# Decoder kernel: four barrier-separated stages of a batch become one program, the output projection moves between two halves of the input projections

## The reference

```python
x = x + mamba(layernorm(x))                 # selective scan, 512 inner channels, 16 states
x = x + attention(layernorm(x), ctx)        # 16 heads: causal self plus cross, one projection Wp
x = x + ffn(layernorm(x))                   # abel = gelu(xn @ W); top-2 of 8 experts; rotation; gate
```

## Time and profile before

| what | us |
|---|---|
| median of 3 runs | 2071.34 (2068.38 to 2071.91) |
| the profiled execution's own time | 2069.24 |
| its span, first to last instruction | 2067.5 |
| PE busy in the span | 1588.2 (77%) |
| DVE busy | 1411.7 (68%) |
| ACT busy | 834.1 (40%) |
| POOL busy | 660.5 (32%) |
| mean granted clock of PE, share of full | 0.878 |

### The profile page before, as it was taken

One profiled execution on the slowest core, in us unless ns is written; L12 is line 12 of the kernel. 1 busy time (PEld: TensorE's weight loads), 2 busy tenths in 40 slices (PEclk: granted clock), 3 DMA queues, 4 the chain that ended last, 5 costly groups with the idle time before them and its releaser, 6 DMA issues. The chain is left out here.

```text
span 2067.5 us, 19892 instructions
## 1 busy us (share of the span) xinstructions
PE 1588.2 (77%) x6792; PEld 757.9 (37%) x6792; DVE 1411.7 (68%) x2092; ACT 834.1 (40%) x1570; POOL 660.5 (32%) x427
## 2 busy tenths in 40 slices
PE   4797699863987699773987799673567899759995
PEld 2454222231544222231544223231233232338884
DVE  5996878465996777276995877277987777234324
ACT  4542156624542166634442266452322466412221
POOL 2653401123663311114653311206654012122221
PEclk9899799985999699976998699886997799859998
DMA  5920721003002720012004520021006320116763
GB/s 170 295 84 13 178 41 20 2 0 129 0 1 66 146 40 1 1 44 86 1 0 115 98 39 2 1 82 42 0 0 144 48 39 2 63 64 220 254 198 124
DMA packets 121189, 147.46 MB, mean 71 GB/s; under 512 B 15429, under 2 KB 103886, under 8 KB 119040
## 3 DMA queue, kind: packets, MB, share of 16 engines
q1 hardware_dynamic: 117344, 137.53, 24.6%
q0 software_dynamic: 3744, 8.66, 1.2%
HBM read 96.79 MB, written 50.79 MB: 71 GB/s over the span
## 5 line engine op out<-in xcount | busy, mean ns | idle before, releaser
L168 PE MATMUL PS<-arena 128*32 128x512 f32 (+11 forms) x4150 | 884.6, 453 | 102.2 <-ACT arena L1698 23.4
L168 PEld LDWEIGHTS PS<-arena 128*32 128x32 f32 (+3 forms) x4150 | 368.5, 128 | 595.6 <-ACT arena L1698 276.0
L1698 ACT ACTIVATE arena<-PS 128x512 f32<-128x512 f32 (+3 forms) x768 | 375.4, 541 | 379.6 <-PE PS L168 378.4
L1328 POOL TENSOR_TENSOR arena<-arena 128x1024 f32<-128x1024 f32 x128 | 302.1, 2361 | 185.9 <-DVE arena L1352 147.1
L1718 DVE TENSOR_REDUCE maxs<-PS 128x1 f32<-128x1024 f32 x256 | 302.2, 1216 | 79.5 <-PE PS L168 79.4
L1352 DVE TENSOR_TENSOR_SCAN arena<-PS,arena 128x1024 f32<-128x1024 f32 x128 | 292.1, 2282 | 9.3 <-POOL arena L1328 9.3
L1308 ACT ACTIVATE PS<-arena,A_neg 128x511 f32<-128x511 f32 x256 | 166.0, 681 | 264.8 <-DVE arena L1352 194.4
L168 PE MATMUL PS<-arena,ident 128*128 128x512 f32 (+1 forms) x560 | 262.2, 595 | 5.4 <-DVE arena L1361 5.4
L1551 POOL TENSOR_TENSOR arena<-xn 128x512 f32<-128x512 f32 x16 | 20.3, 1266 | 586.4 <-ACT xn L1686 586.4
L168 PE MATMUL PS<-bc,bc_sel 96*128 96x512 bf16 x128 | 53.2, 416 | 153.5 <-DVE arena L1361 96.1
L1361 DVE TENSOR_TENSOR arena<-arena,PS 128x1024 f32<-128x1024 f32 x128 | 156.3, 1221 | 7.3 <-PE PS L168 3.2
(11 more groups left out here) (258 smaller groups left out, 1763.4 us busy)
## 6 DMA issues: line engine op xcount, KB each, us to landing
arena<-in_ew SPq DMA_DIRECT2D x46, 512.0 KB
arena<-stack_parts SPq DMA_DIRECT2D x288, 64.0 KB, 4.2
rows_in<-nil SPq DMA_DIRECT2D x16, 1088.0 KB, 12.0
arena<-b_rows SPq DMA_DIRECT2D x16, 1024.0 KB, 7.7
stack_parts<-arena SPq DMA_DIRECT2D x40, 384.0 KB, 3.1
arena<-stack_parts SPq DMA_DIRECT2D x96, 128.0 KB, 4.7
arena<-rows_in SPq DMA_DIRECT2D x23, 272.0 KB, 5.4
arena<-picked_rows SPq DMA_DIRECT2D x16, 256.0 KB, 3.2
```

The source lines that it names most:

```text
L168: return nc.tensor.matmul(o, l, r, start=start, stop=stop)
L1328: nc.gpsimd.tensor_tensor(b_sb[i % 2], u[:, 2 * kh:2 * kh + 2, :], Brow[:, n, :].unsqueeze(1).to_broadcast([P, 2, T]), ALU.mult).then_inc( ...
L1698: nc.scalar.activation(probs[(HG * s + h) % NPR][:, 0:N], bank(4 + n % 2)[:, 0:N], ACT.Exp, scale=HD ** -0.5).then_inc(S["ring_read"], 1)
```

## The change

There is one block a round, in which each engine runs its programs of the stages one after another: `[entry(0), scan(0)]` first, then `[queries(b), attention(b), entry(b + 1), scan(b + 1)]` for each b, the last without a scan. The barriers between queries, attention, entry and scan are gone; the one after the scan stays, and `reset()` stands there now. Where a barrier ordered something, a counter does: the rows in the diff with `wait_ge`. With it come:

- PE: the transposes of the new batch (from a new place, `xnE`) and the first four of the eight groups of input projections stand before `project`, the other four behind it.
- DVE: `normalise` of the new batch stands ahead of the last group's reciprocal, which moves from `attention` to `entry`; `conv(0)` and `conv(1)` stand before `residual`, `conv(2)` between `norm_first` and `norm_second`.
- `inputs` tells `u_ready` after each channel group, and POOL's products of the scan wait for two of them.
- POOL: the eight scatters of a batch stand one behind each of units 1 to 8 of the scan; only after batch 3 are they together. The add of the abel output (L821) is gone; in its place DVE adds it in the experts' phase, one add of 128x1024 a batch.
- Buffers are laid elsewhere (`xn2`, `dots`, the order of `GA2, GA3, GT, GA, GX`), the load of `GX` waits for `ab_mm`, and ACT for `res_added` and `kept` in units 1 and 5 of the scan.

```diff
-        for b in range(NB + 1):
+        def entry(b):
             begins, ends = b < NB, b >= 1
...
         def project():
+            pe.wait_ge(S["y_ready"], NG)
...
-                    if ends:
-                        project()
                     if begins:
-                        to_columns(pe, xn, 0, 0)
-                        pe.wait_ge(S["xT_ready"], 2)
+                    to_columns(pe, xnE, TT * ends, 0)
+                    pe.wait_ge(S["xT_ready"], 2 + 2 * ends)
+                    if ends:
+                        pe.wait_ge(S["ring_read"], ring_den(NG - 1, 1) + 1)
                         for m in range(2 * DT):
+                        if ends and m == DT:
+                            project()
...
-                            last = nc.vector.tensor_tensor(u[:, m, :], delta[:, m, :], xs[:, m, :], ALU.mult)
-                        link(last)
+                        nc.vector.tensor_tensor(u[:, m, :], delta[:, m, :], xs[:, m, :], ALU.mult)\
+                            .then_inc(S["u_ready"], 1)
...
-                        normalise(dve, link, x_sb, xn)
+                    normalise(dve, link, x_sb, xnE)
+                    dve.wait_ge(S["xT_mm"], 2 + 2 * ends)
+                    nc.vector.tensor_copy(xT[:, 1, :], bank(1)).then_inc(S["xT_ready"], 1)
...
-                        residual()
+                    dve.wait_ge(S["den_ready"], NG)
+                    nc.vector.reciprocal(R2, R1).then_inc(S["norm_ready"], 1)
...
+                    conv(0)
+                    conv(1)
...
+                    residual()
                         norm_first()
...
+                    conv(2)
...
+                    if n == 0:
+                        pool.wait_ge(S["u_ready"], 2 * (kh + 1))
...
+                    if b >= 1 and 1 <= i <= TOPK * TT:
+                        scatter(pool, i - 1)
...
-                        pool.wait_ge(S["res_added"], 1)
-                        pool.wait_ge(S["abel_ready"], 1)
-                        nc.gpsimd.tensor_tensor(x1[:], x1[:], ab[:, :, 0:DM], ALU.add).then_inc(S["res_added"], 1)
...
+                    link(nc.vector.tensor_tensor(rest, rest, part[:, :, 0:DM], ALU.add))
...
+        for b in range(-1, NB):
+            stages = [entry(b + 1)] if b < 0 else [queries(b), attention(b), entry(b + 1)]
+            if b + 1 < NB:
+                stages.append(scan(b + 1))
...
+            if b + 1 < NB:
             reset()
```

More of the change, by code:

```diff
@@ new lines, in decoder, with ring, ring_den, scatter @@
+        TILES = [(x, hh, half) for hh in range(2) for x, half in ((0, 0), (1, 0), (2, 0), (3, 0), (3, 1))]
+        CS = 2 * TT
+        STEPS = CS + TT
+        CJOBS = HG * TT
+        JOBS = CJOBS + HG * 2
+        def ring(g, k, h):
+            return HG * (STEPS * g + k) + h + 2 * max(g - 1, 0) + (2 if g >= 1 and k >= 2 else 0)
+        def ring_den(g, i):
+            return HG * STEPS * (g + 1) + 2 * g + i + (2 * HG if g + 1 < NG else 0)
+        def scatter(pool, k):
+            t, j = k // TOPK, k % TOPK
+            if k == 0:
+                pool.wait_ge(S["rows_told"], 4)
+                pool.wait_ge(S["weighed"], 2)
+                pool.wait_ge(S["route_ready"], 1)
+            nc.gpsimd.indirect_dma_start(
+                rows_in, bass.IndirectOffsetOnAxis(ap=route[:, j, t:t + 1].bitcast(I32), axis=0),
+                xn2[:, j, t, :], None).then_inc(rows_stored, 16)
@@ L1507, in max_slot, with attention @@
+        def attention(b):
             def max_slot(g, i):
@@ new lines, in gpsimd @@
+            def gpsimd(pool):
+                all_stored(pool)
+                for i in range(NPAR):
+                    nc.gpsimd.memset(K[i][SK:SR], 1.0).then_inc(S["ones_ready"], 1)
+                    nc.gpsimd.memset(KC[i][SK:SR], 1.0).then_inc(S["ones_ready"], 1)
+                link = chain(pool, S["pool_chain4"])
+                for g in range(NG):
+                    pool.wait_ge(S["ring_read"], ring_den(g, 1) + 1)
+                    nc.gpsimd.tensor_tensor(R1, den_sb[:, 0, :], den_sb[:, 1, :], ALU.mult)\
+                        .then_inc(S["den_ready"], 1)
+                    nc.gpsimd.tensor_tensor(Y1, Y1, den_sb[:, 1, :], ALU.mult)
+                    link(nc.gpsimd.tensor_tensor(Y2, Y2, den_sb[:, 0, :], ALU.mult))
+                    link(nc.gpsimd.tensor_tensor(Y1, Y1, Y2, ALU.add))
+                    pool.wait_ge(S["norm_ready"], g + 1)
+                    nc.gpsimd.tensor_tensor(YT[g], Y1, R2, ALU.mult).then_inc(S["y_ready"], 1)
@@ L1538, in _ @@
[L1538 to L1539 removed]
+                    for program in programs_of(stages, 0):
+                        program(sp)
                 @block.gpsimd
                 def _(pool):
[L1543 to L1547 removed]
@@ L1769, in decoder @@
-            reset()
+                    for program in programs_of(stages, 4):
+                        program(dve)
+            if b + 1 < NB:
+                reset()
 def kernel(**inputs):
```

1715 lines of the change are left out of this document (848 added, 867 removed).

## The result

| | before | changed |
|---|---|---|
| median of the runs, us | 2069.86 (2067.01 to 2071.91, 4 runs) | 2019.55 (2018.02 to 2022.06, 4 runs) |
| the profiled execution's own time | 2069.24 | 2022.06 |
| its span | 2067.5 | 2020.2 |
| mean granted clock of PE | 0.878 | 0.889 |
| first recurrences of the four scans start at | 57.4, 511.0, 965.1, 1419.1 | 59.4, 497.5, 934.5, 1370.4 |

The ratio is 0.9759, 95% interval 0.9741 to 0.9777. Forecast were 2032 us (2014 to 2048) and faster. The kernel gained 50.3 us by the medians and 47.3 by the two spans, where the sum said 38.5. A second set of five runs of the changed kernel gave 2015.77 and 0.9735 (0.9716 to 0.9754), so two medians of one kernel lie 3.8 us apart.

The account below looks back on a forecast made before the run. DVE was taken to pace entry and scan, with engines idle at stage borders. Terms of -18.0, -25.5, +2.8, +4.7 and -2.5 us sum to -38.5: 2069.24 to 2030.7, with 2.1 for the median 2032 us, range 2014 to 2048.

Parts of the forecast that it names:

- Attention to entry to norm: Batches 1 to 3: gains 2.2 before the residual, 5.7 at convolutions, less 1.9 behind PE's new pause; -18.0 us in all.
- Entry to scan: Batches 1 to 3: 12.9 us gained at the border, less 4.4 as POOL's products hold DVE; -25.5 in all.
- Scatters in the scan: Scatters between POOL's products in the scan cost nothing, since the products are ready ahead of DVE's recurrences: 0.
- B: Scan: scatters dearer behind products, 2 us each, losing 12.6 us over three scans; 2045 us, chance 0.15.
- C: Scan: scatters held by DVE's recurrences, 3.6 us each, making the kernel slower; 2078 us, chance 0.06.
- Batch 0: Start of the first scan, without scatters: POOL's early products hold DVE, scan starts at 60.2, +2.8 us.
- Reset: Border behind each of the four scans: PE starts 1.50 us after DVE's end instead of 0.32; +4.7 us.
- Queries to attention: Border between queries and attention: PE waits for loads, not the barrier, so removing it gains 0.
- After batch 3: Last scan to experts: barrier and reset 1.5 us, plus 1.0 from POOL's dropped add; -2.5 us.
- Rival A: Entry to scan: POOL's early products let DVE through, so four holds of 4.4 us vanish; 2014 us, chance 0.10.
- D: Entry: PE at its lower clock in the projections, some 3.5 us a batch lost before the residual; 2042 us, chance 0.12.
- E: Entry gains nothing: convolutions end late or PE's second half of projections delays the chain; 2050 us, chance 0.05.

Follow-up runs that it names:

- experiment 3: Changed kernel with the entry's old order on PE and DVE put back, no barrier added: 2051.32 us, 0.9917 of the kernel before.
- experiment 7: Changed kernel with six idle PE products behind the second half of the input projections: 2027.97 us, 0.9796 of the kernel before.
- experiment 1: Changed kernel, but POOL's second product of a scan waits for the end of DVE's entry: 2006.17 us, 0.9691 of the kernel before.
- experiment 2: Changed kernel, but POOL waits for all four channel groups of u before its first product: 2013.72 us, 0.9731 of the kernel before.
- experiment 9: Changed kernel, but POOL's first two products of a scan both wait for the end of DVE's entry: 2001.82 us, 0.9668 of the kernel before.
- experiment 11: Changed kernel run again without any edit, the second set of runs: 2015.77 us, 0.9735 of the kernel before.
- experiment 6: Changed kernel with the barrier between queries and attention back in all four batches: 2015.85 us, 0.9728 of the kernel before.
- experiment 8: Changed kernel without DVE's four adds of the abel output in the experts' phase: 2015.18 us, 0.9721 of the kernel before.
- experiment 4: Changed kernel with a batch's eight scatters in one run behind the scan's second product: 2022.35 us, 0.9772 of the kernel before.

## Why the prediction was right, and where not

1. *Attention to entry to norm.* Forecast were a start of the projections 1.69 behind the denominators' copy, of the output projection 8.7, the last residual add 15.7; measured 1.62, 8.59, 15.70. The 5.7 at the convolutions measured 6.3 a batch. The term that failed is "so 1.9 are lost": transposes and time-step projections were as slow as put there (6.25 us together, forecast 7.1), but I let PE pace the copy of the time-step inputs, and ACT does. That was a misreading of the kernel before, not only a wrong forecast: the row at 466.62 shows no wait for the projection, ACT was busy until then, and from the columns to the time-step copy it is 3.32 us in both kernels. What follows I had not costed at all. The low stretch of the clock, which had lain on all of the dt products (7.19), moved forward to the transposes, where nobody waits; the last logits come 2.2 to 5.0 sooner. Forecast -18.0, measured -5.6 - 18.8 - 9.6 = -34.0. This is where the forecast fell short. Experiments 3 and 7 show that it is the place of the low stretch: with the old order, or with the pause ahead of the transposes filled, it lies on the dt products again (7.19). With all pauses filled they take 3.70, which the unfilled kernel also has where its second low stretch comes late.
2. *Entry to scan.* Forecast 12.9 less a hold of 4.4, -25.5. Measured -12.66 at the border and +4.16 on u, with 0.12 gained in the routing: -25.9. Experiments 1, 2 and 9 settle the cause: each hold goes with its product, and stands wherever the product does. The held instructions took 2.71 and 2.82, a little more than the 1.5 to 2.5 that I had named. The Trainium skill, "SBUF — State Buffer", section "SBUF: two separate sides", gives the rule for it: an exclusive lock of the port pair that a VectorE instruction with two SBUF inputs and a GpSimd one that reads SBUF share. The rows agree (2.71 and 2.82 for 0.69; 5.04 for 0.79).
3. *Scatters in the scan:* 0, as forecast. They cost 1.01 with 0.16 between, and a unit keeps 3.45. Two rivals ask more: B 2 us for a scatter, C 3.6. The scatter at 502.40 overlapped the recurrence of 500.97 to 503.25 by 0.85 us and was no longer than others. That recurrence reads one input from PSUM. Beside DVE's dot products, which have two SBUF inputs, the first scatter of a batch took 1.19 in both kernels, and each of them its usual 0.43. No run was made with a scatter beside a VectorE instruction in a two-port mode, for which the Trainium skill, "SBUF — State Buffer", section "SBUF: two separate sides", has the writing of descriptors wait.
4. *Batch 0:* forecast 60.2 and +2.8, measured 59.36 and +1.95. The border took 1.60 and the hold 4.15, as put, but the work ahead of it was 0.76 sooner in this profile; in that of experiment 11 the scan starts at 60.4.
5. *Reset:* forecast +4.7. The steps to the first out-projection add sum to 1.34 + 1.69 + 1.52 + 2.07 = 6.6, of which the doubled reset shows 4.7 to be its own. PE starts 1.45 us behind DVE's last gate in each batch, 0.32 before; the other 2.1 lie behind PE's start, where the first out-projection add follows after 3.79 us in batch 1 and took 3.22.
6. *Queries to attention:* 0, and experiment 6 shows no cost.
7. *After batch 3:* forecast -2.5. In the trace it is -1.0 up to the last residual add and -1.9 from there to the experts. In the experts' phase the changed kernel's profile is 4.2 longer, within the upper end (+5.6) that I had kept for DVE's adds. Experiment 8 doesn't pin it on them; the phase varies by 4.1 us among kernels that have the same code there. What causes that stays open.

Rival A (no hold) fell with rows 482.90 and 485.53, B and C with experiment 4 and the scatter's rows, D with an output projection of 7.07, E with experiment 3, which shows the entry's order to be worth 28 us by the trace and 32 to 36 by the medians. By the spans the sum was 8.8 us short. Step 1 gave 16.0 more than forecast, of which the logits are 9.6 (15.2 in experiment 11's profile), the failed loss 5.7; steps 2, 4 and 7 gave 0.4, 0.8 and 0.4 more. Against it stand 1.9 at the reset, 4.2 in the experts and 2.7 in queries and attention of the four batches. The last is -0.3 in experiment 11's profile, so nothing shows it to be the change's. That the total came out nearer than its largest part is luck: step 1 missed by 16.0, and three terms that I had put lower or at nothing hid half of it. What stays open is why the second low stretch of the clock falls on the dt products in one batch (11.89) and behind them in another (9.12).

## What to carry to other kernels

Price a removed barrier from the last engine's end to the next start, and then look at what the engines that are now early do to the one that is late: here POOL's early products cost 4.15 us a batch for 1.1 of use, and one wait gave 14 us back. Place a GpSimd instruction where VectorE waits or reads PSUM (the recurrence kept its 2.28 us beside POOL's products), not where it works on two SBUF inputs. Where PE must pause, arrange the order so that the slow products behind the pause are ones that nobody waits for.

## What the hardware did that I had not expected

- Keeping PE busy in one pause gained nothing and cost up to 4 us an entry (13.3 to 13.6 us to the logits against 9.12 or 11.89): the low clock, which had begun 10.6 us ahead of the time-step copy, began 0.4 behind it, on the path. PE had paused 1.51, 1.12 and 2.05 us ahead of it. Filled pauses right up to the products kept the clock at 1.00.
- The same stretch takes one of two times in the changed kernel, 9.12 or 11.89 us, by where the clock's second low stretch lies. Single profiles of one kernel differ by 7 us in span (2020.2 and 2013.3), as much as several of the edits are worth.
- The hold works both ways, if less: POOL's product took 2.71 and 2.78 instead of 2.34 where it began beside a DVE instruction on u, its copy of the rows 1.43 instead of 1.04.
- Four recurrences over 8 columns were held 4.25 us by two POOL products.
